# A kernel of twelve chained layers: three projections of the next batch tile move to other steps in the two wide cross-attentions

## The reference, cut to what matters

```python
def _L0_xattn_ref(x, context, Wq, Wk, Wv, Wo, bo):
    q = split_heads(x @ Wq)
    k = split_heads(context @ Wk)
    v = split_heads(context @ Wv)
    sim = jnp.einsum('bhid,bhjd->bhij', q, k) * SCALE
    attn = jax.nn.softmax(sim, axis=-1)
    out = jnp.einsum('bhij,bhjd->bhid', attn, v)
    return out @ Wo + bo

x = x + _L0_xattn_ref(_layernorm(x, axis=-1), ctx_768, ...)
...
x = x + _L2_xattn_ref(_layernorm(x, axis=-1), ctx_768, ...)
```

## Time and profile before

| what | value |
|---|---|
| runs | 1691.94, 1692.5, 1696.25 us |
| the profiled execution | 1691.59 us |
| its span | 1689.7 us |
| PE busy | 1527.2 us, 90% |
| DVE busy | 1060.3 us, 63% |
| ACT busy | 830.9 us, 49% |
| POOL busy | 767.7 us, 45% |
| one tile of xattn0, from scores to scores | 39.5 us |
| one tile of xattn2 | 39.1 us |

### The profile page before, as it was taken

How to read it: one execution, slowest core, us unless ns; L and a number is a source line. 1 busy time by engine, 2 the same in 40 slices (tenths; PEclk the granted TensorE clock), 3 DMA queues, 4 the chain that set the end, 5 groups by cost and what they waited for, 6 DMA issues and landing times. The chain is left out here.

```text
span 1689.7 us, 37134 instructions
## 1 busy us (share of the span) xinstructions
PE 1527.2 (90%) x13507; PEld 1317.3 (78%) x13507; DVE 1060.3 (63%) x2934; ACT 830.9 (49%) x2414; POOL 767.7 (45%) x894
## 2 busy tenths in 40 slices
PE   7999999988888999988999999997769697859998
PEld 6899999856567999976899999964459644649997
DVE  5888888556867788865877777749831142353332
ACT  5766666555336787852766666640014122113332
POOL 7665666353339999943211211228823311113332
PEclk9999999999999999998999999999969988969999
DMA  8655554212013333303533333343056272942221
GB/s 259 199 165 175 172 165 150 99 70 83 1 39 101 132 134 132 134 22 102 187 110 111 130 108 108 126 162 100 0 168 182 45 239 90 360 144 33 39 39 26
DMA packets 127222, 204.52 MB, mean 121 GB/s; under 512 B 21034, under 2 KB 92363, under 8 KB 126659
## 3 DMA queue, kind: packets, MB, share of 16 engines
q1 hardware_dynamic: 119016, 188.83, 34.3%
q0 software_dynamic: 6720, 8.79, 3.2%
q10 hardware_dynamic: 1306, 4.51, 0.8%
HBM read 161.76 MB, written 41.14 MB: 120 GB/s over the span
## 5 line engine op out<-in xcount | busy, mean ns | idle before, releaser
L1074 DVE TENSOR_SCALAR xattn_oT<-banks,xattn_last 128x256 f32<-128x256 f32 x254 | 111.1, 479 | 89.8 <-PE banks L854 89.2
L963 ACT ACTIVATE xattn_probs<-banks,xattn_negmax 128x257 f32<-128x257 f32 x256 | 123.3, 482 | 85.4 <-DVE xattn_negmax L1055 85.2
L968 ACT ACTIVATE xattn_probs<-xattn_probs,xattn_rsum 128x257 f32<-128x257 f32 x256 | 131.3, 513 | 1.4 <-DVE xattn_rsum L1059 1.4
L1351 POOL TENSOR_SCALAR xattn_probs<-xattn_probs,xattn_rsum 128x257 f32<-128x257 f32 x128 | 119.4, 933 | 23.9 <-DVE xattn_rsum L1624 23.1
L974 ACT CAST xattn_probsT_hi<-banks 128x256 fp32r<-128x256 f32 x256 | 94.8, 370 | 57.2 <-PE banks L829 57.2
L1055 DVE TENSOR_REDUCE xattn_negmax<-banks 128x1 f32<-128x257 f32 x256 | 106.2, 415 | 13.4 <-PE banks L820 12.0
L1064 DVE TENSOR_TENSOR xattn_probsT_lo<-banks,xattn_probsT_hi 128x256 fp32r<-128x256 f32 x256 | 105.5, 412 | 11.2 <-ACT xattn_probsT_hi L974 10.2
L765 POOL COPY ctx_stat<-xattn_mv 128x2 f32<-128x2 f32 x32 | 6.0, 187 | 225.0 <-DVE xattn_mv L1088 225.0
L829 PE MATMUL banks<-ident,xattn_probs 128*128 128x128 f32 x512 | 101.6, 281 | 6.2 <-ACT xattn_probs L968 5.7
L816 PE MATMUL banks<-xattn_ctxT,xattn_qk_hi 128*128 128x258 f32 x256 | 93.7, 366 | 0.5 <-DVE xattn_qk L1051 0.5
L715 POOL TENSOR_SCALAR xattn_ctxT<-xattn_rawT 128x514 fp32r<-128x514 f32 x32 | 49.9, 1558 | 88.7 <-issue 82.5
(11 more groups left out here) (516 smaller groups left out, 5093.8 us busy)
## 6 DMA issues: line engine op xcount, KB each, us to landing
xattn_ctxT<-ctx_partsT SPq DMA_DIRECT2D x64, 516.0 KB, 4.1
xattn_ctxN<-ctx_partsN SPq DMA_DIRECT2D x64, 384.0 KB, 4.1
ctx_partsT<-xattn_ctxT SPq DMA_DIRECT2D x32, 516.0 KB, 2.7
moe_w<-in_L_ffn_W SPq DMA_DIRECT2D x16, 1024.0 KB, 12.8
ctx_partsN<-xattn_ctxN SPq DMA_DIRECT2D x32, 384.0 KB, 3.5
moecap_w_early<-in_L_ffn_w SPq DMA_DIRECT2D x10, 1024.0 KB, 10.3
xattn_rawN<-in_ctx SPq DMA_DIRECT2D x32, 192.0 KB, 2.7
xattn_raw<-in_ctx SPq DMA_DIRECT2D x32, 192.0 KB, 5.2
```

Of the source, the lines that this page charges most:

```text
L963: nc.scalar.activation(probs[:, n % RING, :], SB[n % 2][:, 0:KV], ACT.Exp, bias=negmax[:, n % RING:n % RING + 1], accum_out=psum[:, n % RI ...
L968: nc.scalar.mul(probs[:, n % RING, :], probs[:, n % RING, :], rsum[:, n % RING:n % RING + 1]).then_inc(norm_ready, 1)
L1074: nc.vector.tensor_scalar(oT[k][:, heads, b, :], by_head(out_banks(n)[k][:, k * 2 * P:(k + 1) * 2 * P]), last[:, k, j * PER_TILE + b:j * P ...
L1351: nc.gpsimd.tensor_scalar(probs[:, n % RING, :], probs[:, n % RING, :], rsum[:, n % RING:n % RING + 1], None, ALU.mult).then_inc(norm_read ...
```

## The change

The table of steps of the folds is changed. Nothing else is.

```diff
@@ -475,7 +475,7 @@
     SPLIT = 10
     PIECES = 4
-    FOLD = (5, 10, 12, 14)
+    FOLD = (5, 7, 9, 12)
     STATISTICS, MOMENTS, ROWS, TURN_NEXT, TAKE_NEXT = (0, 1, 2, 3), 4, (7, 8, 9, 10), 12, (13, 14)
     VALUES, TAKE_VALUES = {7: (0, 1), 9: (2, 3)}, (8, 10)
```

## The result

| | before | changed |
|---|---|---|
| median | 1692.2 us | 1725.0 us |
| lowest to highest, 4 runs each | 1690.8 to 1696.3 | 1718.1 to 1729.1 |
| ratio, with its 95% interval | | 1.020 (1.018 to 1.023) |
| profiled execution, span | 1691.6, 1689.7 | 1728.4, 1726.5 |

The ratio is 34 us of the time before, 5 either way; the medians lie 33 apart. The kernel is slower clear of noise; whether by a little more or a little less than 2% is not settled. Forecast was 1720, with 1711 to 1730 as the range. The windows of one tile of xattn0 with a clock that fell, one with a full clock, and one tile of xattn2 (length, busy PE, PEld, DVE, ACT, POOL, clock) stand against the earlier trace rows.

The account below looks back on a forecast made before the run. PE was taken to bound the kernel. Full tiles at +2.10 (xattn0) and +2.11 (xattn2), six each, gave +25.3; first tiles +2; in all +27.3 on 1691.6, so 1718.9, said as 1720, range 1711 to 1730 (forecast's own 1713 to 1727).

Parts of the forecast that it names:

- PE bounds the two stages: In xattn0 PE is busy 39.12 of 39.52 us a tile, so each microsecond it stands is one of the kernel.
- Wait A: Second fold, in step 7, waits for the first fold's subtractions: 0.61 in xattn0, 1.02 in xattn2, each full tile.
- Wait B: Third fold, in step 9, waits for the second fold's subtractions, written behind `out`: 1.77 in xattn0, 1.37 in xattn2.
- The chain counted from the start of L854: Wait B in xattn0: `out` 0.32 later, first L1051 1.22, second 1.38, fold 0.72; sum 3.64.
- The saving: Folds directly ahead of the values share one entering: 0.14 saved a fold, 0.28 a full tile, ends 0 and 0.56.
- The first tiles: First tile of each stage: no saving, no wait A, B of 1.37; both together put at +2.
- What becomes late next: Transposes in steps 8 and 10 need a normalisation on ACT: taken as 0, upper end 0.4 at each.
- The clock: Rival, 4%: wait B of xattn0 lowers PE's clock in each of 6 tiles, 3.4 lost at a fall: +20, 1740.
- Not slower: Rival, 4%: waits at steps 7 and 9 absent or hidden, only the saving stands: 1685 to 1689.
- half of it: Rival, 6%: DVE's small work slips elsewhere or the two waits share more, about 1.1 a tile: 1707.
- Transposes wait too: Rival, 8%: steps 8 and 10 wait as step 6 does, 0.4 twice in 12 tiles: +10, 1730.

Follow-up runs that it names:

- kernel with early subtractions: Against the changed kernel, DVE's two subtractions of an odd-step fold stand in that same step, ahead of `out`; 1689.5 us, ratio 1.000.
- the one with B of xattn2 longer: Against the changed kernel, DVE adds 352 unread columns between `out` of step 7 and the subtractions in xattn2's six full tiles; 1739.5 us, ratio 1.030.

## Why the prediction was right

Point by point, in its own steps.

- *PE bounds the two stages, so its idle time is the kernel's.* Right: 32 us of waits for folds, and 40 us longer stages.
- *Wait A*, said 0.61 and 1.02: the fold is delayed by 0.63 and 1.04 (printed 0.57 and 0.97). *Wait B*, said 1.77 and 1.37: delayed by 1.91 and 1.48 (printed 1.84 and 1.41). The chain counted from the start of L854 was right in its order; its links came out at 0.32, 1.34 for the 1.22 of the earlier trace rows (163.21 to 164.55), 1.37 for the 1.38 of the earlier trace rows (164.55 to 165.92) and 0.75 for the 0.72 of the earlier trace rows (165.92 to 166.67).
- *The saving*, said 0.14 a fold: 0.16 (step 7 of the kernel with early subtractions is 5.19, before it was 4.11, so a fold beside values adds 1.08; the even step lost 1.24). The values start 1.09 behind the fold's start, with a wait ahead of it (158.74 to 159.83) and without one (149.41 to 150.50), exactly as the transposes did in the earlier trace rows: leaving the fold's tiles for the values' costs what leaving them for the whole array costs. The Trainium skill (TensorEngine Tiling (Array Packing), Key Properties) has it that a change of tiling mode drains the engine. By that rule 0.14 a fold was to be saved and not 0.28, and the trace agrees.
- *The first tiles*, said +2 together: +5.2. The step that failed is the one that costed everything but B there at nothing. B delays the fold by 1.5 in each, 1.37 was said. Beyond that, step 14 grows by 1.0 in xattn0 and 0.4 in xattn2, since transposes wait for DVE's L1064 (1.2 and 0.3); step 11 of xattn2 grows by 0.5, with a new wait of 0.38 for a normalisation, while that of xattn0 loses 0.6, as was expected; step 15 grows by 0.2 in each, and a fold without values beside it adds 1.3 in an odd step where an even one loses 1.2.
- *What becomes late next*, taken at 0, with normalisations named. In the full tiles the normalisations of steps 8 and 10 were never late; L1064 in step 14 of xattn0 was, 0.24 to 0.33 in five of six tiles, and the bare step takes 1.25 to 1.34 instead of 0.83: 2.2 us not foreseen.
- *The clock*, a rival at 4%: it was no rival but a part of the outcome, in 4 of 6 tiles of xattn0, 1.6 each (3.61 less 1.97), 6.5 in all. I had put it as an all-or-nothing case at 3.4 a tile. The rows for it were at hand, 1.82 without a fall, 2.19 with one, but the 1.82 was taken for a length that does not fall. It does at times: the very same wait, L1843 before and L1846 in the kernel with early subtractions, 1.82 in both, is followed by a clock of 1.00 in the one (364.5 to 367 us) and of 0.50 in the other (362 to 364.5).
- *Not slower*, *half of it*: refuted. *Transposes wait too*: not in steps 8 and 10 and not for ACT, as it was put; something of the kind came in step 14 for DVE, at 2 us and not 10.

The sum in the terms of the forecast: A 10.0 (said 9.8), B 20.3 (18.8), saving -3.8 (-3.4), first tiles 5.2 (2), step 14 2.2 (0), clock 6.5 (0): 40.4, against 40.1 measured in the stages and 27.3 forecast. So the two waits and the saving, the heart of the forecast, were right within 2 us, and 12 us were missing from it: the clock, the first tiles and step 14. That the median came within 5 us of 1720 all the same is in part luck: 3.3 us of the profiled execution came back outside the stages, and the median of the four runs lies 3.4 under that execution, whose 1728.4 is above the 1713 to 1727 that the forecast gave itself.

## What to carry to other kernels

Where one bank serves all steps of a kind, the distance that counts is not how many steps lie between two of them, but what the engine that empties the bank has queued ahead of the emptying, and whether that waits for the very engine that will want the bank: here `out` closed a ring. Moving two instructions of DVE ahead of it took the whole loss out of the full tiles and the time back to that of before, where moving PE's work had cost 2%. And a wait should be costed together with what the clock may do behind it, as a chance and not as yes or no, as soon as a wait near its length is seen beside a fall anywhere in the trace.

## What the runs showed of the hardware

- Same wait, both outcomes: over the profiles of four kernels, stretches of 1.82 to 1.85 of idle PE in step 9 went with a fall of the granted clock in 18 of 30 tiles (4, 4, 3 and 4 of 6 in xattn0, 3 of 6 in xattn2), those of 1.40 to 1.43 in none of 30 full tiles. A fall cost 1.6 us: the values behind the wait ran at 1.2 GHz. These are not 30 independent draws: in the changed kernel and in the one with B of xattn2 longer, the same four tiles of xattn0 fell.
- The 1.43 at which none of these tiles fell is no bound for the whole program. A wait of 1.62 in a first tile of xattn0 was followed by a fall. In the profile before, outside the two stages, two waits in a row, of 1.47 (ended at 491.08 us) and 0.97 (ended at 492.93), were followed by a clock of 0.50 from 493.6 to 496.8.
- Leaving the tiles of a fold costs the same whether the values in theirs come next or transposes in the whole array: the next group starts 1.09 behind the fold's start in both cases, where the fold's own pitch would give 0.95.
- 24 runs of the kernel before on one chip lie between 1682 and 1696 us, wider than the three shown before (1691.9 to 1696.3): the 0.3% that I called the bound of what can be told needs a dozen runs of each kernel (12 against 17 to 24 runs gave intervals of 0.2% either way).
